# Third layer norm applied by GpSimd, ahead of its own weight and residual operations, on the table of four places

## What is computed

```python
x = x + 0.5 * ffn(layernorm(x))        # recurrent: 8 steps of a gated cell c, then tanh
x = x + attn(layernorm(x))             # gated delta rule over 1024 tokens, 16 heads of 16
x = x + 0.5 * ffn(layernorm(x))        # the first ffn's weights again
# the end of attn, where the change is made:
static_out = x_act @ W.T
return layernorm(static_out + o_dyn) * o_norm_w + o_norm_b
```

## Time and profile before

| | |
|---|---|
| Median of 3 runs | 1498.38 us (1492.49 to 1502.06) |
| The profiled execution | 1506.1 us, of which the span is 1504.3 us |
| Busy share of the span | PE 91%, DVE 59%, ACT 40%, POOL 18% |
| ACT in L107 (136 tiles) | 70.3 us |
| POOL in L1145 and L1147 (64 tiles each) | 54.6 us and 48.3 us |
| Granted TensorE clock, mean | 0.961 of full |

### The profile page before, as it was taken

How to read it: one execution, slowest core, us unless ns; L and a number is a source line. 1 busy time by engine, 2 the same in 40 slices (tenths; PEclk the granted TensorE clock), 3 DMA queues, 4 the chain that set the end, 5 groups by cost and what they waited for, 6 DMA issues and landing times.

```text
span 1504.3 us, 61982 instructions
## 1 busy us (share of the span) xinstructions
PE 1375.4 (91%) x27811; PEld 1264.2 (84%) x27811; DVE 889.1 (59%) x2208; ACT 602.5 (40%) x1465; POOL 274.0 (18%) x350
## 2 busy tenths in 40 slices
PE   4899999999999999989988989899899999999797
PEld 4889888989989888788877878888889889898786
DVE  2657786868678467468548744943445455454522
ACT  2243433433334334334432533344344545544332
POOL 0022121111211111113303310320311304040500
PEclk9999999999999989899889998999999999999999
DMA  4011111122121332242224233224324243332000
GB/s 133 1 57 57 60 58 64 56 101 75 68 78 67 98 94 79 85 162 71 77 68 139 78 101 123 78 84 133 108 65 149 71 143 84 112 103 94 1 29 29
DMA packets 64201, 125.39 MB, mean 83 GB/s; under 512 B 12352, under 2 KB 33088, under 8 KB 61888
## 3 DMA queue, kind: packets, MB, share of 16 engines
q1 hardware_dynamic: 63936, 121.43, 25.2%
HBM read 62.13 MB, written 59.24 MB: 81 GB/s over the span
## 4 chain that ended last, share of the span: by engine, by line
PE 71%; DVE 16%; issue 5%; ACT 5%; DVEq 0%; ACTq 0%
PE ps L440 35%; PE ps L507 8%; PE ps L1052 7%; PE ps L852 6%; PE ps L1036 4%; PE ps L699 3%; PE ps L671 3%; DVE ln_bn L83 2%; ACT gates L457 2%; PE ps L400 2%; DVE prod L774 2%; DVE inv L777 1%; ACT ffn_rows L107 1%; PE ps L492 1%; PE ps L680 1%
## 5 line engine op out<-in xcount | busy, mean ns | idle before, releaser
L440 PE MATMUL ps<-cst,wt 128*128 128x128 f32 x2688 | 355.6, 285 | 9.2 <-DVE cst L485 8.8
L440 PEld LDWEIGHTS ps<-cst,wt 128*128 128x128 f32 x2688 | 322.5, 195 | 21.1 <-DVE cst L485 10.4
L440 PE MATMUL ps<-ffn_rows,wt 128*128 128x128 f32 x2304 | 305.7, 285 | 15.9 <-ACT gates L457 4.9
L440 PEld LDWEIGHTS ps<-ffn_rows,wt 128*128 128x128 f32 x2304 | 282.3, 197 | 25.1 <-issue 13.6
L479 DVE TENSOR_TENSOR fc<-gates,cst 128x256 f32<-128x256 f32 x112 | 55.2, 493 | 292.5 <-ACT gates L457 292.3
L457 ACT ACTIVATE gates<-ps,colv 128x128 f32<-128x128 f32 x448 | 127.3, 366 | 222.5 <-PE ps L440 222.5
L1052 PE MATMUL ps<-e,kgb 32*128 32x64 f32 x4032 | 127.6, 273 | 3.0 <-issue 2.6
L1052 PEld LDWEIGHTS ps<-e,kgb 32*128 32x128 f32 x4032 | 118.7, 186 | 11.3 <-issue 4.6
L852 PE MATMUL ps<-inv_cols,kv 32*32 32x32 f32 x8192 | 102.2, 198 | 24.8 <-issue 14.5
L1141 POOL TENSOR_TENSOR ffn_rows<-ffn_rows,rowv 128x256 f32<-128x256 f32 x64 | 52.7, 860 | 396.0 <-DMA ffn_rows<-x_scratch 396.0
L852 PEld LDWEIGHTS ps<-inv_cols,kv 32*32 32x32 f32 x8192 | 87.0, 109 | 44.2 <-issue 26.7
(11 more groups left out here) (118 smaller groups left out, 1759.1 us busy)
## 6 DMA issues: line engine op xcount, KB each, us to landing
kg_scratch<-kg_rows SPq DMA_DIRECT2D x32, 512.0 KB, 3.9
xs_scratch<-xs_out SPq DMA_DIRECT2D x32, 512.0 KB, 3.6
xsb<-xs_scratch SPq DMA_DIRECT2D x64, 256.0 KB, 3.4
kgb<-kg_scratch SPq DMA_DIRECT2D x256, 64.0 KB, 2.6
ffn_rows<-x SPq DMA_DIRECT2D x32, 256.0 KB, 3.5
x_scratch<-ffn_rows SPq DMA_DIRECT2D x32, 256.0 KB, 2.8
e_scratch<-e SPq DMA_DIRECT2D x256, 32.0 KB, 1.7
ffn_rows<-e_scratch SPq DMA_DIRECT2D x8, 1024.0 KB, 6.1
```

The costliest lines, as they stand in the source:

```text
L440: mm = pe.matmul(banks[g][:, col:col + P], wt[:, w, k, m * P:(m + 1) * P], rhs, start=(x in (0, FI)), stop=(k == KT - 1 and (t == 0 or x > ...
```

## The change

ACT no longer applies `ln3`: both halves at u = 3 are gone. POOL applies all eight tiles with `apply_pool`, at the head of its own u = 3 work, and then goes on with the weight and residual operations as before.

```diff
@@ -1125,9 +1125,7 @@
             if b is None:
                 return
             tiles = range(4 * half, 4 * half + 4)
-            if u == 3:
-                ln3.apply(act, b.n, xn, xn, tiles)
-            elif u == 6:
+            if u == 6:
                 fg.ln.apply(act, b.n, xn, xt[b.p], tiles)
 
         def post_pool(pool, i):
@@ -1140,6 +1138,7 @@
                 for r in range(8):
                     pool.tensor_tensor(xt[p][:, r, :], xt[p][:, r, :], rowv[:, 2, :], ALU.add).then_inc(post_done, 1)
             if u == 3:
+                ln3.apply_pool(pool, n, xn, xn, range(8))
                 for r in range(8):
                     pool.wait_ge(ln3.applied, 8 * n + r + 1)
                     pool.tensor_tensor(xn[:, r, :], xn[:, r, :], rowv[:, 1, :], ALU.mult).then_inc(post_done, 1)
```

## The result

Nine runs of each kernel: 1506.69 us median after the change (1501.19 to 1512.59) against 1497.93 before (1492.49 to 1507.35). The ratio is 1.0058, with a 95% interval of 1.0029 to 1.0086: 4.3 to 12.9 us more, most likely 8.7. The profiled execution after took 1509.89 us (span 1508.1, mean clock 0.957); that of before took 1506.1 (span 1504.3, clock 0.961), so the two spans differ by 3.8 us.

A forecast was written before the change was run, and what follows sets the result against it. PE, busy 91% of the span, was taken as the full engine, so work counts only where PE waits. Terms -3.2 - 0.2 + 4.4 + 3.4 = +4.4 us on 1498.4 gave 1502.8 us, range 1490 to 1509.

The forecast's parts named there:

- The gains: PE's lost time given back, mainly at u = 3: 3.2 us in blocks 0 to 6, 0.2 kept in block 7.
- The 0.60 of blocks 0 and 1: PE's wait for `zbd` behind the late gates, 0.30 us in each of blocks 0 and 1, would go.
- Block 2's 0.39: In block 2 the second half of the tiles delays the copy of `e`; PE's 0.39 us wait would go.
- POOL's price: POOL needs about 17.7 us from coefficients to last residual row; hidden in blocks 0 to 6, not in block 7.
- Block 7: Of 4.5 us gained at u = 3, 0.2 are kept; DVE waits 4.2 us for POOL at u = 5.
- The collision: Blocks 0 and 1: POOL's work meets DVE's `rms` chain, L785 comes 2.2 us later and PE waits, 4.4 together.
- The clock: Behind PE's longer gaps in blocks 0 and 1 a low clock costs 1.7 us each, 3.4 for both.
- Chains that do not meet: Rival: POOL is through before `rms` starts, or DVE has slack; only the gains stay, 1495.0 us; chance 0.28.
- The stall without the clock: Rival: PE's gaps in blocks 0 and 1 come without a lower clock, 1499.4 us; chance 0.15.
- A whole POOL operation for each collision: Rival: in the `rms` chain each collision costs 0.72 us, 3.0 per block instead of 2.2; 1504.5 us; chance 0.08.
- POOL as the bound at u = 5 of every late block: Rival: DVE waits for POOL at u = 5 in every late block, 14.1 us, 1516.9 in all; chance 0.04.

The follow-up runs named there:

- the sixteen are held back: The change, with POOL waiting in blocks 0 and 1 between the eight tiles and its sixteen operations until DVE finished the rms chain: 1499.69 us, ratio 1.0003.
- POOL in blocks 0 and 1: Against the change: POOL applies the norm in blocks 0 and 1 only, ACT keeps it in blocks 2 to 7: 1511.15 us, ratio 1.0078.
- DVE late: The kernel before, with one extra DVE reduction into an unused tile between rms and L785 in blocks 0 and 1: 1511.14 us, ratio 1.007.
- the change once more: The changed kernel, unaltered, measured again beside the other experiments on the same chip: 1512.2 us, ratio 1.0067 against before.

## Why the prediction was right, step by step

The forecast was 1502.8 us, 4.4 more than before, in a range of 1490 to 1509. The median came to 1506.69, inside it, and within 1% of before. The difference, 8.7, is twice the 4.4, which lies at the lower end of its interval: the way and the mechanism were right, the size was not.

- **The gains.** Blocks 4 to 6 were put at 1.37 + 0.10 + 0.78 = 2.25 and gave 2.27, 2.5 with their next steps. The 0.60 of blocks 0 and 1 can be seen where the sixteen are held back: 0.44 each. Block 2's 0.39 is there too, in u = 4: its row stands in that step (982.68 to 993.69) and not in u = 3, as the heading there says. PE's wait for `e` is gone after the change, and it stays at 0.36 and 0.39 in the two kernels in which ACT keeps block 2's norm (POOL in blocks 0 and 1, and DVE late). Those two also show how far the gain of blocks 4 to 6 varies: their u = 3 took 10.59, 9.75 and 9.57, and 9.60, 9.15 and 9.92, which is 3.5 and 2.3 us over the change's.
- **POOL's price.** 17.7 us from the coefficients to the last row: the timeline of block 7 has 1421.97 - 1404.30 = 17.67. Hidden in blocks 4 to 6, as forecast: in block 4 POOL is through 4.6 us before DVE needs it (3.8 forecast).
- **Block 7.** The stall went where the forecast had put it, into DVE's wait at u = 5. It was put at 4.2 and was 2.91, DVE being that much later itself; the statistics start 17.8 us after the coefficients, against 18.0 before. Instead of 0.2 kept, 0.47 were lost: the term that the sum lacks is the clock behind PE's gap, now twice as long (0.71 more in L507).
- **The collision.** It was put at 2.2 us per block, by 5.2 operations at +0.41. The price of one was right (+0.42 to +0.55), the number was not: POOL made its sixteen at 0.79 each to the end and met one operation of the chain in block 0, three in block 1: 0.44 and 1.40 us instead of 2.2. But in both blocks L589 ended 0.5 us later in its step than before, since DVE's L483 ahead of it met POOL too (0.93 and 0.99 instead of 0.43 before), and PE came to its wait 0.5 earlier, having lost its own idle time ahead of it. So the gaps came out near the forecast by errors that cancel, which is luck: 2.9 forecast; 2.14 and 3.17 in the change's profile, 3.0 to 3.6 in the four others of this arrangement. The sums are thereby not a proof of the working; the experiments are, since holding POOL back removes the gap, and a late DVE without POOL makes it.
- **The clock.** 1.7 per gap was forecast, 1.56 is in the windows of both. In the three other profiles with such gaps, u = 3 and u = 4 together show 1.5 and 1.2 (the change once more), 1.4 and 2.5 (DVE late), and 1.3 and nothing (POOL in blocks 0 and 1): 1.4 in the mean of the eight, but the single gap is not forecast by it. Left out of the sum is what lies beside it, the 3 us that only the runs' mean clocks show.
- **The rivals.** Chains that do not meet: refuted by the rows of block 1. The stall without the clock: refuted in the change's own windows (0.86 behind both gaps), though one gap of another kernel passed so. A whole POOL operation for each collision: the rows of `rms` show +0.42 to +0.55, less than the 0.72 of one. The page "SBUF — State Buffer" of the Trainium skill, section "Who interferes with whom", calls the port pair that DVE and GpSimd share an exclusive lock, and says of DVE's 2-port modes that the engine which comes second fully blocks. The rows agree with a wait for the rest of one POOL operation: each of the four ended 0.08 to 0.14 us behind POOL's. POOL as the bound at u = 5 of every late block: only in block 7.

## What to carry to other kernels

Work moved to an idle engine costs little for its own length and much for what it meets: look for the chain on the other engines that it will run beside, and for the short operation at that chain's end that frees a buffer for the full engine. A gap of 2 to 3.5 us on that engine cost itself and, in seven of the eight seen here, 1.2 to 2.5 us more in clock, so it is worth moving the buffer-freeing operation ahead of a part of the chain, or splitting the work so that it ends sooner. But not the whole chain behind it: what stood behind the chain is then late instead.

## What the runs showed of the hardware that was not expected

A run of POOL operations that do not wait for one another can keep a DVE operation with two inputs out until the run is over, not only for the one operation that is under way: 4.46, 9.91 and 10.85 us for an operation of 0.43, beside 8 to 16 POOL operations at 0.68 us each. It does not always: in the other blocks the two took turns, and so they did in the change beside the eight independent additions of `o_norm_b` (L1139) in block 7, where the same DVE operation took 0.94. Where each POOL operation waited for the one before it (0.79 each), DVE came in between, at +0.42 to +0.55. The section of the Trainium skill named above speaks of a lock for the whole instruction; these rows show a DVE operation kept out over a run of them, in some of the blocks only. Two of the operations that met POOL in `rms`, L57 and L59, read a single tile.
